# A fused adaLN block on one core: Down units cast behind the group's snapshots, a half chunk one group earlier, one weight load earlier, and a new order of the start

## The reference

```python
mod = (silu(c) @ wmod).reshape(1, 6, 1, -1)         # sa, ca, ga, sb, cb, gb
ga, gb = sign(ga) * max(|ga|, 0.25), sign(gb) * max(|gb|, 0.25)
h = layernorm(x) * (1 + ca) + sa
x = x + ga * (h @ (weight * blockmask).T + bias)    # 1024 x 1024, blocks of 32 x 32
h = layernorm(x) * (1 + cb) + sb
x = x + gb * down(silu(gate(h)) * up(h))            # weights int32 with a scale per row
```

## Time and profile before

| what | us |
|---|---|
| median of 3 runs | 1204.59 (1204.57 to 1208.73) |
| the profiled execution | 1207.13 |
| its span, first to last instruction | 1205.3 |
| mean granted clock of TensorE | 0.971 |
| busy: TensorE / VectorE / GpSimd / ScalarE | 1112.7 / 764.2 / 468.7 / 427.2 |

### The profile page before, as it was taken

How to read it: one execution, slowest core, us unless ns; L and a number is a source line. 1 busy time by engine, 2 the same in 40 slices (tenths; PEclk the granted TensorE clock), 3 DMA queues, 4 the chain that set the end, 5 groups by cost and what they waited for, 6 DMA issues and landing times.

```text
span 1205.3 us, 13075 instructions
## 1 busy us (share of the span) xinstructions
PE 1112.7 (92%) x4629; PEld 517.5 (43%) x4629; DVE 764.2 (63%) x966; ACT 427.2 (35%) x776; POOL 468.7 (39%) x453
## 2 busy tenths in 40 slices
PE   5989999999999799999888989898988899999998
PEld 3544544545444344444333434343433344444444
DVE  3879948767677777687667667767525234444344
ACT  0322047555564443554445444544324100000000
POOL 1033326647563563647566574747422000000000
PEclk8999899999999999999999999998998999999999
DMA  9983222334625645447465455465355965545540
GB/s 350 401 309 75 72 69 81 78 86 149 230 63 162 149 131 166 133 133 197 121 179 161 149 167 178 143 174 163 104 208 224 377 244 229 215 191 191 191 191 36
DMA packets 94288, 206.93 MB, mean 172 GB/s; under 512 B 18576, under 2 KB 54160, under 8 KB 91792
## 3 DMA queue, kind: packets, MB, share of 16 engines
q1 hardware_dynamic: 78176, 145.81, 37.2%
q0 software_dynamic: 16048, 60.30, 14.7%
HBM read 137.39 MB, written 68.68 MB: 171 GB/s over the span
## 4 chain that ended last, share of the span: by engine, by line
PE 37%; POOL 8%; DMA 6%; ACT 2%; issue 2%; DVE 2%; ACTq 0%; DVEq 0%; POOLq 0%
PE pA L1286 12%; PE pA L1353 11%; PE pB L1353 8%; PE pB L1286 4%; DMA down_scratch<-work 3%; POOL work L848 1%; POOL work L846 1%; POOL work L845 1%; DMA down_left_scratch<-work 1%; POOL work L843 1%; ACT work L1056 1%; DMA h_left_scratch<-work 1%; POOL work L815 1%; POOL h_scratch L829 1%; POOL work L813 1%
## 5 line engine op out<-in xcount | busy, mean ns | idle before, releaser
L1286 PE MATMUL pA<-work 128*128 128x512 f16 x1680 | 398.1, 392 | 52.9 <-ACT work L1032 46.4
L1286 PEld LDWEIGHTS pA<-work 128*128 128x128 f16 x1680 | 166.8, 100 | 270.9 <-ACT work L1032 55.8
L1152 PE MATMUL pA<-work 128*128 128x512 f32 x512 | 228.2, 601 | 2.8 <-ACT work L929 1.1
L1286 PE MATMUL pB<-work 128*128 128x512 f16 x752 | 176.9, 380 | 4.8 <-DVE work L1717 4.8
L1739 DVE SCALAR_TENSOR_TENSOR work<-work 128x512 f16<-128x512 f16 x144 | 128.2, 894 | 39.3 <-ACT work L1050 38.7
L1152 PEld LDWEIGHTS pA<-work 128*128 128x128 f32 x512 | 96.8, 193 | 117.3 <-issue 113.8
L1353 PE MATMUL pA<-work 128*128 128x512 f16 x600 | 136.1, 382 | 4.9 <-DMA work<-down_left_scratch 4.9
L1032 ACT ACTIVATE work<-pA 128x512 f32<-128x512 f32 x126 | 74.8, 594 | 142.3 <-PE pA L1286 135.0
L907 ACT ACTIVATE work<-pB,small 128x128 f32<-128x128 f32 x256 | 92.6, 480 | 84.1 <-PE pB L1141 77.6
L829 POOL DMA_DIRECT2D h_scratch<-work x80 | 61.6, 780 | 149.9 <-DVE work L1739 147.9
L1286 PEld LDWEIGHTS pB<-work 128*128 128x128 f16 x752 | 73.6, 98 | 94.3 <-DVE work L1717 6.2
(11 more groups left out here) (173 smaller groups left out, 1140.3 us busy)
## 6 DMA issues: line engine op xcount, KB each, us to landing
work<-h_scratch SPq DMA_DIRECT2D x8, 4480.0 KB, 13.7
h_scratch<-work POOLq DMA_DIRECT2D x60, 512.0 KB, 3.9
work<-in_L_wmod SPq DMA_DIRECT2D x10, 2048.0 KB, 18.7
work<-in_L_ffn_gate_w SPq DMA_DIRECT2D x84, 128.0 KB, 3.5
work<-in_L_ffn_up_w SPq DMA_DIRECT2D x84, 128.0 KB, 3.1
work<-down_scratch SPq DMA_DIRECT2D x7, 1280.0 KB, 11.2
work<-in_L_ffn_down_w SPq DMA_DIRECT2D x68, 128.0 KB, 4.1
work<-in_L_attn_data SPq DMA_DIRECT2D x16, 512.0 KB, 4.3
```

Of the source, the lines that this page charges most:

```text
L1152: last = pe.matmul(pA[:, 2 * par(t) + h, :], hT1[par(t)][:, c, :], wT[:, c, h * H:(h + 1) * H], start=(c == 0), stop=(c == KT - 1))
L1286: last = pe.matmul(ps, w[:, m, c], bc[b][:, mv_, s, c], start=begin, stop=(i == n - 1 and c == KT // 2 - 1 and s == 1), skip_group_check=True)
```

## The change

- Down units: ScalarE casts the unit of g-1 behind all high parts of g-1, before the cast of g's gate or up unit, rather than before the second silu; VectorE turns g's unit at the end of its step. Down units start in group 13 rather than 14.
- The half chunk's first run stands before group 38 rather than 39. There are two output buffers, and a half waits for the store of the half before the last.
- The leftover weights `wl` get a place of their own, and their load no longer waits for the last S4 store. Some buffers of Down move with it.
- The start: SP loads all mask and weight tiles before piece 4, and piece 5 after two blocks of x. VectorE sums the second mask group before the halves of row 2, with the norm of block 2 between these. TensorE mixes `turn_rows` into the attention of block 1, and the gate row follows `attend(0, 1)`. Columns 3 and 4 move behind the first half of block 5 and the bound products into its second half, in another bank.

```diff
@@ -166,7 +166,7 @@
...
         tail_silu = at(o, 4 * H)
-        tail_out = at(o + 4 * H, 2 * H, F16)
+        tail_out = [at(ot, 2 * H, F16) for ot in (o + 4 * H, O_GA + 24 * H)]
         assert o + 6 * H <= O_GA
@@ -188,12 +188,14 @@
...
         wd = [at(O_WD[m], SLICE_W, F16).rearrange("p (q i d) -> p i q d", q=4, i=NPR) for m in range(NC)]
-        wl = at(O_TRNB, 2 * 6 * H, F16).rearrange("p (c k d) -> p c k d", c=2, k=3)
-        io = [at(O_WC + 4 * H * k, 4 * H) for k in range(4)]
-        tmp = [at(O_WC + 4 * H * (4 + k), 4 * H) for k in range(2)]
-        dsnap = [at(O_WC + 4 * H * (6 + k), 4 * H) for k in range(3)]
-        assert HB + 2 * SLICE_W <= O_WC and O_HL[0] + 12 * P <= O_GBS and O_WC + 4 * H * 9 <= O_STG
-        assert O_SLICE + SLICE_W <= O_GA and O_TRNB + 12 * H <= O_S4 and O_HL[1] + 12 * P <= O_X1
...
+        O_WL = O_WC + SLOT_B
+        wl = at(O_WL, 2 * 6 * H, F16).rearrange("p (c k d) -> p c k d", c=2, k=3)
+        io = [at(o, 4 * H) for o in (O_WC, O_WC + 4 * H, O_WC + 8 * H, O_WL + 12 * H)]
+        tmp = [at(O_WL + 4 * H * (4 + k), 4 * H) for k in range(2)]
+        dsnap = [at(O_X1 + 4 * H * k, 4 * H) for k in range(3)]
+        assert HB + 2 * SLICE_W <= O_WC and O_HL[0] + 12 * P <= O_GBS and O_WL + 24 * H <= O_STG
+        assert O_SLICE + SLICE_W <= O_GA and 12 * H <= O_WL - O_WC and O_HL[1] + 12 * P <= O_X1
@@ -253,8 +255,8 @@
...
         colp = pB[:, 2, 0:2 * KT]
-        colp2 = pA[:, 3, 0:2 * KT]
-        boundT, boundp = pA[:, 3, P:2 * P], pA[:, 3, 3 * P:3 * P + 4]
+        colp2 = pA[:, 0, 0:2 * KT]
+        boundT, boundp = pA[:, 0, P:2 * P], pA[:, 0, 3 * P:3 * P + 4]
         sump = [pB[:, 3, 4 * NB * g:4 * NB * (g + 1)] for g in range(2)]
@@ -384,7 +386,7 @@
...
-        TAIL_BEFORE = {GROUPS.index((FT - SK, 1)): 0, NG - 2: 1}
+        TAIL_BEFORE = {GROUPS.index((FT - 1, 0)): 0, NG - 2: 1}
         NWC = 4
@@ -396,7 +398,7 @@
...
         NDN = len(DOWN)
-        DOWN_FROM = 14
+        DOWN_FROM = 13
         turned_in = {}
@@ -581,13 +583,12 @@
...
                     sp.dma_start(wst[r], w_v[r]).then_inc(w_loaded[r], 16)
-                if g == 0:
-                    load_piece(4)
-                    load_piece(5)
+            load_piece(4)
             for i in range(2):
...
                 load_x(i + 2)
+            load_piece(5)
             load_piece(6)
@@ -659,7 +660,6 @@
...
             load_wd(WT1)
-            sp.wait_ge(s4_stored, 16 * stores_before(NG, S4))
             sp.dma_start(wl.rearrange("p c k d -> p (c k d)"), wl_d.rearrange("p c k d -> p (c k d)")).then_inc(wl_loaded, 16)
@@ -860,7 +860,7 @@
...
                 pool.wait_ge(tail_ready, 2 * blk + half + 1)
-                pool.dma_start(hl_v[blk, half][:, :, 2 * P:3 * P], tail_out.rearrange("p (j t) -> p j t", j=NJ)).then_inc(tail_stored, 16)
+                pool.dma_start(hl_v[blk, half][:, :, 2 * P:3 * P], tail_out[half].rearrange("p (j t) -> p j t", j=NJ)).then_inc(tail_stored, 16)
@@ -1062,12 +1062,13 @@
...
                     act.wait_ge(tail_ready, n)
-                    act.wait_ge(tail_stored, 16 * n)
+                if n >= 2:
+                    act.wait_ge(tail_stored, 16 * (n - 1))
                 ps = tail_bank[half]
...
                 act.wait_ge(tail_prod_ready, n + 1)
-                act.activation(tail_out[lo_h], ps[up_h], ACT.Copy, scale=1.0 / LO)
-                act.activation(tail_out[up_h], ps[up_h], ACT.Copy, scale=1.0 / LO).then_inc(tail_hi_ready, 1)
+                act.activation(tail_out[half][lo_h], ps[up_h], ACT.Copy, scale=1.0 / LO)
+                act.activation(tail_out[half][up_h], ps[up_h], ACT.Copy, scale=1.0 / LO).then_inc(tail_hi_ready, 1)
@@ -1091,9 +1092,6 @@
...
                 if g:
-                    for u in turned_in[g - 1]:
-                        if u in dn_index:
-                            cast_unit(u)
                     silu_of(g - 1, 1)
@@ -1114,6 +1112,10 @@
...
                     hi_of(g - 1, m)
+                if g:
+                    for u in turned_in[g - 1]:
+                        if u in dn_index:
+                            cast_unit(u)
                 if g < NG:
@@ -1142,7 +1144,7 @@
...
             def attend(t, h, ks=range(KT)):
-                if h == 0:
+                if h == 0 and ks[0] == 0:
                     pe.wait_ge(hT1_ready, t + 1)
@@ -1232,33 +1234,32 @@
...
             pe.wait_ge(wT_ready, 4)
-            attend(0, 0)
-            attend(1, 0, range(0, 4))
+            attend(0, 0, range(0, 3))
             mask_total_of(1)
-            attend(1, 0, range(4, KT))
+            attend(0, 0, range(3, KT))
+            turn_rows(4)
+            for n in range(5, KT):
+                attend(1, 0, range(2 * n - 10, 2 * n - 8))
+                turn_rows(n)
+            attend(1, 0, range(6, KT))
+            pe.wait_ge(wT_ready, 2 * KT - 4)
+            attend(0, 1)
             pe.wait_ge(mask_bits, 2)
...
             gate_row(2, rowp[0])
-            for n in range(4, KT):
-                turn_rows(n)
-            pe.wait_ge(wT_ready, 2 * KT - 4)
-            attend(0, 1)
             transpose(0, 2)
...
             for t in range(2, NT + 1):
+                if t == 6:
+                    pe.wait_ge(bma_copied, 1)
+                if t <= LAST:
+                    attend(t, 0)
                 if t == 5:
...
-                    attend(t, 0, range(0, 3))
-                    pe.wait_ge(bounds_in, 4)
-                    pe.transpose(boundT[0:4, :], bmx, ident).then_inc(bounds_turned, 1)
-                    attend(t, 0, range(3, 6))
-                    pe.wait_ge(bounds_max, 2)
-                    pe.matmul(boundp, one[0:4].to_broadcast([4, P]), bdiag[0:4], start=True, stop=True)\
-                      .then_inc(bounds_out, 1)
-                    attend(t, 0, range(6, KT))
-                elif t <= LAST:
-                    attend(t, 0)
+                    pe.wait_ge(pair_free, 3)
+                    for v in (3, 4):
+                        columns(v, colp2[:, KT * (v - 3):KT * (v - 2)])
                 if t <= LAST - 1:
@@ -1266,13 +1267,17 @@
...
                 if t == 5:
-                    pe.wait_ge(bma_copied, 1)
-                if t <= LAST:
...
+                    attend(t, 1, range(0, 4))
+                    pe.wait_ge(bounds_in, 4)
+                    pe.transpose(boundT[0:4, :], bmx, ident).then_inc(bounds_turned, 1)
+                    attend(t, 1, range(4, 6))
+                    pe.wait_ge(bounds_max, 2)
+                    pe.matmul(boundp, one[0:4].to_broadcast([4, P]), bdiag[0:4], start=True, stop=True)\
+                      .then_inc(bounds_out, 1)
+                    attend(t, 1, range(6, KT))
+                elif t <= LAST:
                     attend(t, 1)
-                if t == 4:
-                    pe.wait_ge(pair_free, 2)
-                    for v in (3, 4):
-                        columns(v, colp2[:, KT * (v - 3):KT * (v - 2)])
                 if t in END:
@@ -1583,10 +1588,10 @@
...
                 dve.tensor_copy(*move_rows(u)).then_inc(wT_by_dve, 1)
-            for h in range(2):
-                sum_half(2, h)
             mask_rows_of(1)
+            sum_half(2, 0)
             norm1(2)
+            sum_half(2, 1)
@@ -1757,7 +1762,7 @@
...
                 dve.wait_ge(tail_hi_ready, n + 1)
-                dve.scalar_tensor_tensor(out=tail_out[up_h], in0=tail_out[up_h], scalar=-LO, in1=ps[up_h],
+                dve.scalar_tensor_tensor(out=tail_out[half][up_h], in0=tail_out[half][up_h], scalar=-LO, in1=ps[up_h],
                                          op0=ALU.mult, op1=ALU.add).then_inc(tail_ready, 1)
@@ -1803,9 +1808,6 @@
...
                 if g < NG:
-                    for u in turned_in[g]:
-                        if u in dn_index:
-                            turn_unit(u)
                     dve.wait_ge(p5_done, g + 1)
@@ -1831,6 +1833,10 @@
...
                     lo_of(g - 1, outs[4])
+                if g and g < NG:
+                    for u in turned_in[g]:
+                        if u in dn_index:
+                            turn_unit(u)
                 if g - SLICE_GROUP in range(KT):
```

## The result

| | before | after |
|---|---|---|
| median of 4 runs each, same chip | 1206.66 (1204.57 to 1209.02) | 1158.05 (1155.59 to 1159.41) |
| ratio | | 0.9594 (0.9563 to 0.9625) |
| span of the profiled execution | 1205.3 | 1153.8 |
| TensorE's mean granted clock | 0.971 | 0.985 |

A forecast was written before the change was run, and what follows sets the result against it. TensorE, busy 92% of the span, was taken as the bound, its holes and low clock as savable. Terms -42.4 + 1.5 - 10.8 - 6.6 - 5.2 = -63.5 us took the median from 1204.6 to 1141.0; range 1129 to 1168.

The forecast's parts named there:

- The signs that failed: Profile signs: line 1032 waits from group 16 under 8 us, none over 2; TensorE waiting about 5 near 111.
- Six such cycles: 6 us left of 48.4, a gain of 42.4: Groups 16 to 38, moved casts: only a 0.5 to 1 us hole every fourth group remains.
- The row after 2.50: TensorE's 32 matmuls took 7.08 us after a 2.50 hole; holes of 0.5 to 1 us counted too short to cost clock.
- The start group: Group 13's last slot also holds the first Down turn, 1.24; hole of 1.70 grows to 2.9, costed +1.5 us.
- The half chunk and the weights: Before Down: second buffer removes a wait, -10.8 us; preloaded weights remove the wait of Down's second product, -6.6 us.
- The start: Start until the group stage: holes and low clock removed, less new low clock from waiting for VectorE: -5.2 us.
- 2.5 us in all: VectorE's gain in the start: waits of 0.84 and 3.29 go, gate's clamp comes 1.6 later.
- rival 1: Groups: the wait only changes place, near casts held by the store with snapshot 1 behind; 1160 us, chance 0.17.
- Rival 2: Odd groups: VectorE becomes the bound, one more 1.2 before each gate sum; +12, 1153 us, chance 0.10.
- Rival 3: End gives nothing back, loads collide at Down's start: -5 instead of -17.4; 1153 us, chance 0.07.
- rival 5: Groups: change fails because snapshot 2 was late for another reason; chance 0.06 together with Rival 4.
- Rival 4: Groups: slower, the far cast, sums, store, near cast loop closes later; 1212 us, chance 0.06 together with rival 5.

The follow-up runs named there:

- Experiment 6: Changed kernel with A11/A12 high and low parts written to one of two output buffers by group parity: 1144.05 us, ratio 0.9462.
- Experiments 4 and 11: 4: changed kernel with Down units from group 14 instead of 13, 1167.73 us; 11: the edit of experiment 6 with Down from 14, 1167.57 us.
- experiment 9: Changed kernel, start reordered: normalisations before half-row sums, GpSimd's 1/sigma before its bias additions, columns 3, 4 and bound products later in block 5: 1151.82 us.
- Experiment 2: Also `e_end`: kernel before with only the half chunk one group earlier, two tail buffers and leftover weights loaded early: 1188.23 us, ratio 0.9848.
- Experiment 8: Changed kernel with GpSimd's second bias addition of the start put behind the 1/sigma of block 0: 1159.81 us, ratio 0.9587.
- experiment 5: Changed kernel with VectorE's turn of a Down unit in the next step, behind the product of gate and up: 1160.98 us, ratio 0.9615.
- experiment 1: Kernel before with only the Down casts and turns moved, Down units still from group 14: 1184.48 us, ratio 0.9808.
- experiments 7 and 10: 7: changed kernel with the edits of experiment 5 and Experiment 6, 1143.66 us; 10: those two plus the edit of experiment 9, 1140.04 us.

## Why the prediction was right or wrong

The direction, the order of the terms and the range (1129 to 1168) held; the sum was 17 us too low (1141.0 against 1158.05). Of the 17, 2.1 is the kernel before, whose median moved from 1204.59 to 1206.66 with a fourth run, and 12.0 is what the stage table shows: 10.0 in groups 16 to 38, 0.9 in groups 6 to 15, 1.3 in the start; the last 2.9 are the difference between the profiled executions and the medians. The signs that failed: nine waits for line 1032 with 11.5 us in all and two over 2 (8 and none had been named), and 8.5 us instead of 5 near 112. The others came as named.

- **The casts.** The mechanism was right: the near casts left snapshot 2's way and snapshot 1 was in time. The size was not. The step that failed is "Six such cycles: 6 us left of 48.4, a gain of 42.4": 16.5 were left. I looked for what a late down_scratch store does to the cast that waits for it, and that stayed hidden as forecast. The same store stands in GpSimd's queue ahead of the stores of the output buffers, and ScalarE's high part of A11 waits for one of those, ahead of snapshot 2. Before the change it waited 10.6 us for such stores; that the rest was covered by the larger wait is my reading, which no run tests. Experiment 6 shows the cause: without the wait 12.8 us of the 16.5 are gone. The row after 2.50, by which I took short holes to be free of clock, is no bound either: 2.39 and 2.53 cost 1.7 each.
- **The start group.** I costed `DOWN_FROM` only in group 13: +1.5, measured +2.4, because the hole of 2.83 did take clock (x32 in 8.46). What I missed is far larger: it moves the far unit's four sums out of the step with the chunk's four. Experiments 4 and 11 show 9.7 us with one output buffer and 23.5 with two. My working of the landing still had the four sums for a new chunk in the same step, as in the trace of before, and saw no cost in the odd group's sums being late, for which VectorE and TensorE wait there. Over groups 16 to 38 the traces give 48.9 us lost before, 27.0 with the casts alone and 16.5 with the start group too: 21.9 and 10.5. That the 32.4 measured came as near to 42.4 as it did is luck: a third of it is a term that I had at +1.5. The +1.5 itself hangs on a meeting of VectorE and GpSimd: with the same turn in the same place, experiment 9's hole is 1.60.
- **The half chunk and the weights.** -10.8 and -6.6 against -10.9 and -6.7 by the traces. Experiment 2 has them together at 18.8. Cost and mechanism were right.
- **The start.** -5.2 against -1.9 alone (-3.9 in the trace, less the 1.7 that was there before). The step that failed is VectorE's "2.5 us in all": what I counted as gained idle time had been the time in which GpSimd's two additions ran. Now they meet the normalisation (2.94 instead of 1.99) and the residual's product (3.36 instead of 1.21), 3.1 us, so VectorE is 0.4 later instead of 2.5 earlier and TensorE waits 8.5 and not 5. Experiment 8 shows that this meeting only moves, experiment 9 that part of the hole was order. The three parts alone and the start group add up to 52.9 us (22.5, 18.8, 1.9 and 9.7), the whole gave 48.6; each ratio's interval is 2 to 4 us to either side, so the 4.3 are not shown to be more than noise.
- **The rivals.** In the changed kernel rival 1's place did not come true: the near cast's wait did not reach snapshot 1. It was right that the store's landing keeps its price; the one who pays is another. Rival 2 explains two holes of the nine (1.32, and 1.31 at 716); experiment 5 shows them worth nothing by themselves. Rival 3 is excluded by experiment 2, rival 5 by experiment 1. Rival 4's end, a lost loop, did not come; the nearest to it is the kernel with 14.

What stays open: why the h_scratch store at 562.45 took 7.9 us, and whether the 3.6 us between experiments 7 and 10 are real. Group 14's gain in experiment 9 is read from single traces; no run moves that meeting by itself.

## What to carry to other kernels

When a wait is moved off the path, list everyone who waits for a transfer of the same queue, not only the instruction that was seen waiting: the next one in line was hidden by it. For work that comes every second step, the parity against the other such work is a term of the sum, and a large one; moving its start by one is not "one step earlier". Idle time of VectorE in which GpSimd works is not free time: moved into it, two operations grew by 3.1 us here. Count what the other engine does in it.

## What the runs showed of the hardware that I had not expected

- A store of 512 KB on GpSimd's queue took 4.0 us at the median, and 7.9 when issued 2.9 us after one of 896 KB and soon after two more of h_scratch.
- Two VectorE operations took 2.94 and 3.36 us beside GpSimd's two additions (5.10 in all). Before, at the end of the additions and behind them, they took 1.99 and 1.21. With one addition moved, the time came back elsewhere as 1.97.
- The same hole can cost clock or not. In front of the same product, the kernel before and `e_end`:

```profile
575.46 8.77 PE L1286 MATMUL pA<-work 128*128 128x512 f16 x32 [3.83 <-ACT work L1032]
...
574.54 7.08 PE L1288 MATMUL pA<-work 128*128 128x512 f16 x32 [3.83 <-ACT work L1033]
```

- One start can come at different times: TensorE's same transposes stand at 112.08 to 115.46 us in the profiles of six kernels with the same start, both ends from the same chip. For changes of 2 us the stages have to be counted from a row inside the trace.
